# A buffer of its own for ScalarE's part of the last channel, 6144 of its columns on VectorE by integer range reduction and a monic polynomial, and the channels' outputs summed group by group

## The chip, the cores and the metric

The kernel runs on one core of a Trainium2 chip. The metric is the device time of one launch in microseconds. The kernel before took 3671.42 us (median of 3 runs, 3670.53 to 3673.81).

## The reference

An attention layer over 8 sequences of 512 rows and 128 features (16 heads of dimension 8), followed by a residual sum, layer norm and a feed-forward stage with a shared expert and eight selected experts. The attention repeats its softmax for 16 "wavelength" channels that share Q, K and V:

```python
def wl_step(acc, wl):
    cpm, iw = wl
    m = cpm[None, :, None, None]
    scores = jnp.einsum('bhqd,bhkd->bhqk', Q * m, K * m) * SCALE
    scores = scores * jnp.cos(KERR * scores * scores)
    attn = jax.nn.softmax(scores, axis=-1)
    out = jnp.einsum('bhqk,bhkd->bhqd', attn, V)
    return (acc + out * iw, None)
acc, _ = jax.lax.scan(wl_step, acc0, (cos_pm, interference_weights))
combined = acc / WL_CHANNELS
```

A channel differs from another only by a factor per head on the scores (cos squared, tile `c2`), so the kernel computes the scores of a head once and takes 16 exponentials of them with 16 scales. The cosine of the scores is 1 for these inputs; a flag computed at run time picks the branch without it.

## The kernel before, in words

The eight sequences are two groups of four (`g` = 0, 1). A **unit** `u` is one head of one group, so there are 32. Its scores lie transposed in `s_t[:, p, :]`, 128 partitions by 8192 columns (4 key tiles `kt` x 4 sequences x 512 queries), with `p = u % 2`; the row maximum is already in them. A unit has 16 **waves** `w`, one for each channel, and each engine walks through them in an order written out by hand, kept in step by counting semaphores.

- ScalarE (L583 to L598): for each wave one ACTIVATE Exp of `s_t` into `probs[:, w % 2, :]`, a ring of two buffers, with the channel's scale from a register. It waits until wave w-2's products are done (`pv_done`, L594). Of wave 15 it takes only columns 4096 to 8191.
- TensorE (L1188 to L1220): for each wave 16 matmuls (27 output rows for each of four sequences side by side, 512 columns) of `probs` with V. Three channels are a **group** `wg` and share a PSUM bank, so there are 6 groups, the last with one channel. `prep_pe` puts the next unit's work between the waves: its projections at step 1, row scores at 2 to 5, transposes at 6, the transposed scores at 8 to 11. `turn_products` transposes a group's products, one group late; it waits until the group before is weighted (`norm_done`).
- VectorE (L1378 to L1398): for a group's last wave the copy of its PSUM bank to `o_sb`; `prep_dve`, the other half of the next unit's preparation (copies, row maxima); `weigh(wg)`, which divides a group's products by their sums and multiplies by the channel's weight, into its place of `weighted` [P, 16, 128]; and at the unit's end one tensor_reduce over the 16 channels into `comb`.
- VectorE also computes exp for columns 0 to 4095 of wave 15, the **pieces** (`piece_dve`, L659): four pieces of 1024 columns (two sequences of a key tile), each by range reduction with the constant 1.5 x 2^23 and a polynomial of degree 6, in three parts that are laid at the steps in `PIECE_STEPS`. TensorE's `piece_pe` multiplies them with V into the last group's bank at steps 4, 8, 11, 15 (`PRODUCT_STEPS`). `piece_ready` and `piece_used` guard the one tile `x_p` that they share.
- In the second group of sequences (`g` = 1) the feed-forward stage for finished rows of the first is laid between the waves (`FF_STEPS`, steps counted over a pair of units): stages 1 to 3 at steps 12, 13, 15 of the even unit, stages 4 to 7 at steps 0, 7, 11, 12, 13 of the odd one. Stages 6 and 7 on TensorE wait for VectorE's stages 5.5 and 6.
- GpSimd copies the next unit's weights once per unit; SyncE issues the loads and stores. The second group's transposed x is stored early in DRAM from `x_next`, which lies in `weighted`, and loaded when the first group is through.

After the loop comes a tail: the rest of the feed-forward stage and the experts.

Of the kernel before, what the change touches and what calls it, by code (L numbers as in the profile page):

```python
# [6 lines left out]
ALU = mybir.AluOpType  # L7
ACT = mybir.ActivationFunctionType
AX = mybir.AxisListType
# [38 lines left out]
BIASED_MAGIC = float(1.5 * 2 ** 23 + 127)  # L48
LOWEST_Y = -126.0
EXP2 = (1.0000000005541674, 0.6931472057372656, 0.24022646890630472, 0.05550328776967869, 0.009618488957523083,  # L50
        0.00133999312182961, 0.00015345811891707452)
# [36 lines left out]
def postln_kernel(nc, a):  # L88
    with ExitStack() as ctx:
# [12 lines left out]
        weighted = sb("weighted", [P, W, GT * D])  # L102
        x_next = weighted[:].rearrange("p w n -> p (w n)")
# [105 lines left out]
        x_sq = sb("x_sq", [P, NT + 1])  # L209
# [15 lines left out]
        cos_small = sb("cos_small", [P, 3, NB])  # L225
# [8 lines left out]
        def products_of(wg):  # L234
# [11 lines left out]
                 "qa_ready st_done st_copied exp_done pv_done o_copied ot_done rz_done norm_done comb_done prep_chain chain "  # L246
# [306 lines left out]
        def _(act):  # L553
# [105 lines left out]
        def piece_dve(dve, piece, part, u, p, h):  # L659

            n = u * PIECES + piece
            link = Linked(dve, s["piece_chain"], n * PART_LINKS[3] + PART_LINKS[part])

            a = [c * (-1) ** i for i, c in enumerate(EXP2)]

            def horner(*coefficients):
                for c in coefficients:
                    link(nc.vector.scalar_tensor_tensor(out=x_p[:], in0=x_p[:], scalar=c, in1=x_y[:], op0=ALU.add, op1=ALU.mult))  # L668
# [21 lines left out]
        def piece_pe(pe, piece, u, p):  # L690

            pe.wait_ge(s["piece_ready"], u * PIECES + (piece + 1))
# [3 lines left out]
            kt, b0 = piece * X_BATCHES // NB, piece * X_BATCHES % NB  # L696
# [446 lines left out]
        def _(pe):  # L1143
# [28 lines left out]
            with pe.If(fast == 1):  # L1172
                for g in range(NG):
                    with pe.Fori(g * H // 2, (g + 1) * H // 2) as i:
                        for p in range(2):
# [12 lines left out]
                            for w in range(W):  # L1188
# [8 lines left out]
                                for kt in range(DVE_KT if w == W - 1 else 0, T):  # L1197
                                    for b in range(NB):
# [3 lines left out]
                                            probs[:, w % 2, at:at + S], start=(kt == 0 and w in FIRST_OF),  # L1202
# [40 lines left out]
        def _(dve):  # L1243
            nc.vector.memset(half_pi[:], float(np.pi / 2))
            nc.vector.memset(comb[:, NT - 3:NT - 1, :], 0.0).then_inc(s["sw3_zeroed"], 1)
# [68 lines left out]
            for step in range(W):  # L1314
# [4 lines left out]
                if step == 1:  # L1319
# [3 lines left out]
                    nc.vector.memset(r_z[:], 0.0).then_inc(s["pv_done"], 2)  # L1323
                    nc.vector.memset(loop_chunk.var, 0.0).then_inc(s["norm_done"], 1)
                    nc.vector.memset(loop_chunk.nt, 0.0).then_inc(s["y2_ready"], 1)
# [110 lines left out]
```

## Time and profile before

| | |
|---|---|
| median of 3 runs | 3671.42 us |
| profiled execution, its own time | 3674.77 us |
| its span | 3672.7 us, mean granted TensorE clock 0.882 |
| ScalarE busy | 3476.3 us (95%) |
| VectorE busy | 2934.6 us (80%) |
| TensorE matmuls busy | 2688.7 us (73%) |
| GpSimd busy | 55.8 us (2%) |

Busy shares are over the whole span. A row of a group gives the line, the engine, the operation, what is written and read, and how often. Where work is shown in order of time, neighbours of one kind are merged into one row, and the brackets give the engine's idle time ahead of it and what ended it.

### The profile page before, as it was taken

To read this page: it belongs to the slowest core of one execution; us is meant where nothing else is said; L and a number is where in the kernel's file an instruction comes from. 1 tells how busy PE (TensorE), PEld (TensorE's weight loads), DVE (VectorE), ACT (ScalarE), POOL (GpSimd) and SP (SyncE) were. 2 spreads that over 40 slices of the span, in tenths; PEclk is the share of its full clock that TensorE was granted. 3 is DMA by queue.
4 is the path that set the end of the run, shared out by engine and by line. 5 is a ranking of instruction groups with operands and counts; after the bars stand their busy time and mean duration, and the time that the engine had idled before them with its cause. 6 is when DMAs were issued, how large, how long until landed. Compare 5 with 4: busy or idle time off the path is not lost.

```text
span 3672.7 us, 50238 instructions
## 1 busy us (share of the span) xinstructions
PE 2688.7 (73%) x19639; PEld 823.7 (22%) x19639; DVE 2934.6 (80%) x3858; ACT 3476.3 (95%) x635; POOL 55.8 (2%) x206
## 2 busy tenths in 40 slices
PE   5777777777777777777777777777777777777673
PEld 2222222222222222222222222222222222222222
DVE  6788777788777788777788888788888888888787
ACT  6999999999999999999999999999999999999971
POOL 0000000000000000000000000000000000000000
PEclk7988988888889889888889898889888888988986
DMA  1000000000000000000000000000000000000000
GB/s 46 1 1 1 1 1 1 1 1 1 1 1 1 1 1 1 1 14 1 1 2 1 4 2 4 2 4 1 2 4 2 4 2 1 4 2 4 2 26 29
DMA packets 19221, 16.65 MB, mean 5 GB/s; under 512 B 4177, under 2 KB 16866, under 8 KB 18722
## 3 DMA queue, kind: packets, MB, share of 16 engines
q1 hardware_dynamic: 18130, 12.54, 1.2%
q8 instruction: 185, 3.03, 0.3%
q14 instruction: 58, 0.48, 0.0%
q10 hardware_dynamic: 720, 0.34, 0.0%
q0 software_dynamic: 128, 0.26, 0.0%
HBM read 7.76 MB, written 5.37 MB: 4 GB/s over the span
## 4 chain that ended last, share of the span: by engine, by line
ACT 53%; issue 27%; PE 9%; DVE 4%; ACTq 4%; DMA 0%; POOL 0%; DVEq 0%; POOLq 0%
ACT probs L597 53%; PE psum L1200 7%; ACTq L590 3%; DVE x_p L668 1%; PE psum L719 1%; DVE m_pad L770 0%; ACTq L594 0%; DVE x_p L686 0%; DVE probs L843 0%; PE psum L699 0%; DVE probs L1106 0%; DVE q_s L654 0%; DVE q_t L762 0%; ACT probs L614 0%; DVE k_s L654 0%
## 5 line engine op out<-in xcount | busy, mean ns | idle before, releaser
L597 ACT ACTIVATE probs<-s_t 128x8192 f32<-128x8192 f32 (+1 forms) x512 | 3440.8, 6807 | 69.2 <-PE psum L1200 67.6
L1200 PE MATMUL psum<-probs,v_pad 128*27 128x512 f32 x15872 | 2239.1, 691 | 578.7 <-ACT probs L597 523.0
L1200 PEld LDWEIGHTS psum<-probs,v_pad 128*27 128x27 f32 x15872 | 568.4, 119 | 1976.5 <-issue 1382.2
L668 DVE SCALAR_TENSOR_TENSOR x_p<-x_p,x_y 128x1024 f32<-128x1024 f32 x640 | 782.0, 1222 | 14.2
L1385 DVE COPY o_sb<-psum 128x512 f32<-128x512 f32 x192 | 132.7, 691 | 249.9 <-PE psum L1200 237.5
L791 DVE COPY s_t<-psum 128x2048 f32<-128x2048 f32 x130 | 297.0, 2284 | 11.2 <-PE psum L749 10.2
L770 DVE TENSOR_REDUCE m_pad<-psum 128x4 f32<-128x2048 f32 x132 | 301.6, 2286 | 3.9
L699 PE MATMUL psum<-x_p,v_pad 128*27 128x512 f32 x512 | 157.1, 696 | 190.1 <-DVE x_p L686 190.1
L761 DVE TENSOR_SCALAR v_t<-psum,b_head 128x512 f32<-128x512 f32 x33 | 24.8, 751 | 208.1 <-PE psum L719 208.1
L686 DVE SCALAR_TENSOR_TENSOR x_p<-x_p,x_2k 128x1024 f32<-128x1024 f32 x128 | 156.8, 1225 | 4.4
L1184 PE MATMUL psum<-ident,o_sb 128*128 128x128 f32 x768 | 122.1, 282 | 47.9 <-DVE weighted L1373 47.9
L679 DVE SCALAR_TENSOR_TENSOR x_y<-x_p,x_y 128x1024 f32<-128x1024 f32 x128 | 156.0, 1219 | 0.0
L1395 DVE TENSOR_REDUCE comb<-weighted 128x2048 f32 x32 | 121.3, 3792 | 5.2 <-DVE weighted L1373 5.2
L675 DVE TENSOR_SCALAR x_p<-x_y 128x1024 f32<-128x1024 f32 x128 | 88.9, 695 | 38.3 <-PE psum L699 30.3
L1368 DVE RECIPROCAL r_z<-psum 128x48 f32<-128x48 f32 x192 | 80.6, 420 | 40.8 <-PE psum L1184 37.2
L729 PE MATMUL psum<-k_s,q_s 24*128 24x512 f32 x528 | 67.7, 503 | 62.2 <-DVE k_s L654 40.0
L1184 PEld LDWEIGHTS psum<-ident,o_sb 128*128 128x128 f32 x768 | 82.8, 140 | 104.7 <-issue 104.0
L1373 DVE TENSOR_TENSOR weighted<-psum,r_z 128x384 f32<-128x384 f32 x192 | 98.5, 513 | 6.7
L672 DVE TENSOR_SCALAR x_y<-s_t,c_last 128x1024 f32<-128x1024 f32 x128 | 95.3, 744 | 1.6 <-issue 1.3
L719 PE MATMUL psum<-x_group,w_head 128*32 128x512 f32 x792 | 92.8, 602 | 0.0
L681 DVE TENSOR_SCALAR x_p<-x_y 128x1024 f32<-128x1024 f32 x128 | 88.9, 695 | 4.4
L677 DVE TENSOR_SCALAR x_2k<-x_p 128x1024 int16<-128x1024 int16 x128 | 88.9, 694 | 4.4
(244 smaller groups left out, 990.8 us busy)
## 6 DMA issues: line engine op xcount, KB each, us to landing
x_next_dram<-weighted SPq DMA_DIRECT2D x1, 1024.0 KB, 3.9
x_group<-x_next_dram SPq DMA_DIRECT2D x1, 1024.0 KB, 4.9
loop_memory<-in_L_attn_x_dram SPq DMA_DIRECT2D x8, 128.0 KB, 2.1
x_dram<-loop_memory SPq DMA_DIRECT2D x8, 128.0 KB, 1.8
out_dram<-loop_memory SPq DMA_DIRECT2D x8, 128.0 KB, 1.8
x_dram<-probs SPq DMA_DIRECT2D x2, 512.0 KB, 3.6
out_dram<-probs SPq DMA_DIRECT2D x2, 512.0 KB, 3.6
s_t<-in_L_ffn_ew_dram SPq DMA_DIRECT2D x3, 256.0 KB
```

Source lines behind the costliest of these rows:

```text
L597: nc.scalar.activation(probs[:, w % 2, n0:], s_t[:, p, n0:], ACT.Exp, scale=scales[w % 2]).then_inc(s["exp_done"], 1)
L668: link(nc.vector.scalar_tensor_tensor(out=x_p[:], in0=x_p[:], scalar=c, in1=x_y[:], op0=ALU.add, op1=ALU.mult))
L679: link(nc.vector.scalar_tensor_tensor(out=x_y[:], in0=x_p[:], scalar=BIASED_MAGIC, in1=x_y[:], op0=ALU.subtract, op1=ALU.subtract))
L686: nc.vector.scalar_tensor_tensor(out=x_p[:], in0=x_p[:], scalar=a[0], in1=x_2k[:], op0=ALU.add, op1=ALU.mult).then_inc(s["piece_ready"], 1)
L699: last = nc.tensor.matmul(products_of(NWG - 1)[L * b:L * b + SLOTS * A, :], v_pad[:, p, b * T + kt, VPAD:VPAD + SLOTS * A], x_p[:, i * S:( ...
L719: last = nc.tensor.matmul(prep[L * b:L * b + L, i, :], w_head[:, p, i, :], x_group[:, b * S:(b + 1) * S], start=True, stop=True)
L770: nc.vector.tensor_reduce(m_pad[:, qt, :].rearrange("p (b l) -> p b l", l=L)[:, :, R_S:R_S + 1], banks(qt), AX.X, ALU.max, negate=True).th ...
L791: nc.vector.tensor_copy(s_t[:, p, kt * NB * S:(kt + 1) * NB * S], banks(kt).rearrange("p b q -> p (b q)")) \
L1184: last = nc.tensor.transpose(psum[:, 6, qt * P:(qt + 1) * P], o_sb[:, wg % 2, qt * P:(qt + 1) * P], ident[:])
L1200: last = nc.tensor.matmul(products_of(wg)[L * b:L * b + SLOTS * A, :], v_pad[:, p, b * T + kt, c0:c0 + SLOTS * A], probs[:, w % 2, at:at + ...
L1385: nc.vector.tensor_copy(o_sb[:, wg % 2, :], products_of(wg)).then_inc(s["o_copied"], 1)
L1395: nc.vector.tensor_reduce(comb[:, bass.ds(g * GT, GT), bass.ds((u - g * H) * D, D)].rearrange("p (b t) e -> p t b e", b=NB), weighted[:].r ...
```

## The change

- `DVE_KT` goes from 2 to 3 key tiles: VectorE takes columns 0 to 6143 of wave 15 and ScalarE the last 2048. There are three pieces of 2048 columns (a key tile of all four sequences), in five parts; TensorE takes them at steps 6, 12, 15.
- ScalarE's part of wave 15 goes to a tile of its own, `probs_last`, with no wait ahead of it, and has a bias `ln_k`. The 15 other waves use the ring of two by `(p + w) % 2`.
- A piece: `tensor_scalar` multiplies the scores by the scale, clamps and writes int16 (the rounding gives the integer part); the difference is the fraction; a second `tensor_scalar` makes the bits of 2^n; the polynomial of degree 5 has leading coefficient 1 (all others, and ScalarE's part by its bias, are scaled alike, and the division by the sum takes the factor out).
- `weigh` writes group 0 into `summed` and each later group into `weighted`, which is then added to `summed`; the unit's end adds the three slots.
- `x_next`, `x_sq` and `cos_small` move to other tiles, and the descriptor scratch is given as 4096.

```diff
-DVE_KT = 2
-X_BATCHES = 2
-X_COLS = X_BATCHES * S
-PIECES = DVE_KT * NB // X_BATCHES
+DVE_KT = 3
+X_COLS = NB * S
+PIECES = DVE_KT
...
-PART_LINKS = (0, 4, 7, 9)
-PIECE_STEPS = {0: (0, 0), 2: (0, 1), 3: (0, 2), 4: (1, 0), 5: (1, 1), 7: (1, 2), 8: (2, 0), 9: (2, 1), 10: (2, 2),
-               11: (3, 0), 12: (3, 1), 13: (3, 2)}
-PRODUCT_STEPS = {4: 0, 8: 1, 11: 2, 15: 3}
+LN_K = float(np.float32(-np.log(EXP2[5])))
+K_EXP2 = tuple(c * float(np.exp(LN_K)) for c in EXP2[:5])
+PART_LINKS = (0, 2, 3, 4, 5, 6)
+PIECE_STEPS = {0: (0, 0, 2), 2: (0, 2, 3), 3: (0, 3, 4), 4: (0, 4, 5),
+               5: (1, 0, 1), 7: (1, 1, 3), 8: (1, 3, 4), 10: (1, 4, 5),
+               11: (2, 0, 1), 12: (2, 1, 3), 13: (2, 3, 5)}
+PRODUCT_STEPS = {6: 0, 12: 1, 15: 2}
...
-        weighted = sb("weighted", [P, W, GT * D])
-        x_next = weighted[:].rearrange("p w n -> p (w n)")
+        probs_last = sb("probs_last", [P, (T - DVE_KT) * NB * S])
+        weighted = sb("weighted", [P, SLOTS, GT * D])
+        summed = sb("summed", [P, SLOTS, GT * D])
+        x_next = x_p[:]
+        x_n = x_2k[:].bitcast(I16)
+        ln_k = sb("ln_k", [P, 1])
...
-                                act.wait_ge(s["pv_done"], u * W + (w + 1))
-                                n0 = DVE_KT * NB * S if w == W - 1 else 0
-                                nc.scalar.activation(probs[:, w % 2, n0:], s_t[:, p, n0:], ACT.Exp,
+                                if w == W - 1:
+                                    nc.scalar.activation(probs_last[:], s_t[:, p, DVE_KT * NB * S:], ACT.Exp, bias=ln_k[:, 0:1],
+                                                         scale=scales[w % 2]).then_inc(s["exp_done"], 1)
+                                    continue
+                                act.wait_ge(s["pv_done"], u * W + (w + 2 if w > 1 else w + 1))
+                                nc.scalar.activation(probs[:, (p + w) % 2, :], s_t[:, p, :], ACT.Exp,
                                                      scale=scales[w % 2]).then_inc(s["exp_done"], 1)
...
             if part == 0:
-                scores = s_t[:, p, piece * X_COLS:(piece + 1) * X_COLS]
-                link(nc.vector.tensor_scalar(x_y[:], scores, c2_last[:, bass.ds(h, 1)], LOWEST_Y, ALU.mult, ALU.max))
+                dve.wait_ge(s["piece_ready"], n + 1)
+                link(nc.vector.tensor_scalar(x_n, scores, scale, LOWEST_Y, ALU.mult, ALU.max))
+                link(nc.vector.scalar_tensor_tensor(out=x_y[:], in0=scores, scalar=scale, in1=x_n, op0=ALU.mult, op1=ALU.subtract))
+            if part == 1:
+                nc.vector.tensor_scalar(x_n, x_n, 127.0, 128.0, ALU.add, ALU.mult)
                 dve.wait_ge(s["piece_used"], n + 1)
-                link(nc.vector.tensor_scalar(x_p[:], x_y[:], BIASED_MAGIC, None, ALU.add))
-                low_halves = x_p[:].bitcast(I16).rearrange("p (n o) -> p n o", o=2)[:, :, 0:1]
-                nc.vector.tensor_scalar(x_2k[:].bitcast(I16).rearrange("p (n o) -> p n o", o=1), low_halves, 7, None,
-                                        ALU.logical_shift_left)
-                link(nc.vector.scalar_tensor_tensor(out=x_y[:], in0=x_p[:], scalar=BIASED_MAGIC, in1=x_y[:],
-                                                    op0=ALU.subtract, op1=ALU.subtract))
-                link(nc.vector.tensor_scalar(x_p[:], x_y[:], a[6], None, ALU.mult))
-            if part == 1:
-                horner(a[5], a[4], a[3])
+                link(nc.vector.scalar_tensor_tensor(out=x_p[:], in0=x_y[:], scalar=K_EXP2[4], in1=x_y[:], op0=ALU.add, op1=ALU.mult))
             if part == 2:
-                horner(a[2], a[1])
-                nc.vector.scalar_tensor_tensor(out=x_p[:], in0=x_p[:], scalar=a[0], in1=x_2k[:],
+                horner(K_EXP2[3])
+            if part == 3:
+                horner(K_EXP2[2])
+            if part == 4:
+                horner(K_EXP2[1])
+                nc.vector.scalar_tensor_tensor(out=x_p[:], in0=x_p[:], scalar=K_EXP2[0], in1=x_2k[:],
                                                op0=ALU.add, op1=ALU.mult).then_inc(s["piece_ready"], 1)
...
-            for i in range(X_BATCHES):
-                b = b0 + i
-                last = nc.tensor.matmul(products_of(NWG - 1)[L * b:L * b + SLOTS * A, :], v_pad[:, p, b * T + kt, VPAD:VPAD + SLOTS * A],
-                                        x_p[:, i * S:(i + 1) * S], start=(kt == 0), stop=False)
+            for b in range(NB):
+                last = nc.tensor.matmul(products_of(NWG - 1)[L * b:L * b + SLOTS * A, :], v_pad[:, p, b * T + piece, VPAD:VPAD + SLOTS * A],
+                                        x_p[:, b * S:(b + 1) * S], start=(piece == 0), stop=False)
...
+                                dst = (weighted if wg else summed)[:, 0:n, :]
+                                dve.wait_ge(s["sum_done"], u * NWG + max(wg, 1))
                                 nc.vector.tensor_tensor(
-                                    weighted[:, w0:w0 + n, :].rearrange("p r (j d) -> p j r d", d=D), ot[:, :, :, 0:D],
+                                    dst.rearrange("p r (j d) -> p j r d", d=D), ot[:, :, :, 0:D],
                                     rz.rearrange("p j (r o) -> p j r o", o=1).broadcast_to([P, GT, n, D]),
                                     ALU.mult).then_inc(s["norm_done"], 1)
+                                if wg:
+                                    dve.wait_ge(s["norm_done"], n1 + 1)
+                                    nc.vector.tensor_tensor(summed[:, 0:n, :], summed[:, 0:n, :], dst, ALU.add) \
+                                        .then_inc(s["sum_done"], 1)
...
-                            nc.vector.tensor_reduce(
+                            dve.wait_ge(s["sum_done"], u * NWG + NWG)
+                            nc.vector.tensor_tensor(weighted[:, 0, :], summed[:, 0, :], summed[:, 1, :], ALU.add) \
+                                .then_inc(s["sum_done"], 1)
+                            dve.wait_ge(s["sum_done"], u * NWG + (NWG + 1))
+                            nc.vector.tensor_tensor(
                                 comb[:, bass.ds(g * GT, GT), bass.ds((u - g * H) * D, D)].rearrange("p (b t) e -> p t b e", b=NB),
-                                weighted[:].rearrange("p w (t b d) -> p t b d w", t=T, b=NB), AX.X, ALU.add) \
+                                weighted[:, 0, :].rearrange("p (t b d) -> p t b d", t=T, b=NB),
+                                summed[:, 2, :].rearrange("p (t b d) -> p t b d", t=T, b=NB), ALU.add) \
                                 .then_inc(s["comb_done"], 1)
+                            dve.wait_ge(s["comb_done"], u + 1)
```

## Rows read from the trace of the kernel before

**Rows 1.** The page, part 1: busy us (share of the span) xinstructions.

```profile
PE 2688.7 (73%) x19639; PEld 823.7 (22%) x19639; DVE 2934.6 (80%) x3858; ACT 3476.3 (95%) x635; POOL 55.8 (2%) x206
```

**Rows 2.** ScalarE's groups by shape: busy us, mean ns | idle before.

```profile
L597 ACT ACTIVATE probs<-s_t 128x8192 f32<-128x8192 f32 x480 | 3328.7, 7021 | 69.2 <-PE psum L1200 67.6 <-DVE s_t L791 1.6
L597 ACT ACTIVATE probs<-s_t 128x4096 f32<-128x4096 f32 x32 | 115.3, 3602 | 0.0
...
L561 ACT ACTIVATE probs<-probs,half_pi 128x256 f32<-128x256 f32 x1 | 0.5, 508 | 2.7 <-DVE probs L1259 2.7
L634 ACT ACTIVATE probs<-probs 128x256 f32<-128x256 f32 x1 | 0.4, 416 | 10.2 <-DVE probs L1019 10.2
```

**Rows 3.** ScalarE in order of time: start us, us, work [idle before <-releaser].

```profile
51.25 13.96 ACT L597 ACTIVATE probs<-s_t 128x8192 f32<-128x8192 f32 x2 [1.55 <-DVE s_t L791]
...
1692.27 107.45 ACT L597 ACTIVATE probs<-s_t 128x8192 f32<-128x8192 f32 x16 [1.78 <-PE psum L1200]
...
2132.59 27.81 ACT L597 ACTIVATE probs<-s_t 128x8192 f32<-128x8192 f32 x4 [1.77 <-PE psum L1200]
...
2176.59 65.93 ACT L597 ACTIVATE probs<-s_t 128x8192 f32<-128x8192 f32 x10 [2.14 <-PE psum L1200]
...
3494.60 65.91 ACT L597 ACTIVATE probs<-s_t 128x8192 f32<-128x8192 f32 x10 [0.66 <-PE psum L1200]
3573.53 0.60 ACT L607 ACTIVATE probs<-psum 128x512 f32<-128x512 f32 x1 [13.02 <-PE psum L804]
```

**Rows 4.** ScalarE's waits: us in total, times, longest us.

```profile
ACT probs L597 <- PE psum L1200: 67.6, 43, 2.1
```

**Rows 5.** TensorE in order of time at a unit boundary, columns as in rows 3.

```profile
1687.04 5.57 PE L1200 MATMUL psum<-probs,v_pad 128*27 128x512 f32 x34 [3.29 <-ACT probs L597]
...
1692.88 1.89 PE L1200 MATMUL psum<-probs,v_pad 128*27 128x512 f32 x12
...
1696.86 0.63 PE L1184 MATMUL psum<-ident,o_sb 128*128 128x128 f32 x4 [1.50 <-DVE weighted L1373]
1699.43 5.33 PE L1200 MATMUL psum<-probs,v_pad 128*27 128x512 f32 x32 [1.95 <-ACT probs L597]
1706.28 3.64 PE L1200 MATMUL psum<-probs,v_pad 128*27 128x512 f32 x32 [1.52 <-ACT probs L597]
```

**Rows 6.** Stretches of one unit: us, PE, PEld, DVE, ACT, POOL busy, clock, DMA.

```profile
1692.27:1801.49 109.22, 81.89 (x604) 24.05 (x600) 84.45 (x92) 107.44 (x16) 0.74 (x5) 0.89 0.00 1
...
3122.59:3231.76 109.17, 82.19 (x610) 24.52 (x606) 89.21 (x119) 107.47 (x17) 2.53 (x8) 0.89 0.02 5
3231.76:3341.05 109.29, 83.08 (x615) 25.36 (x611) 94.61 (x145) 107.66 (x18) 0.74 (x5) 0.89 0.00 1
```

**Rows 7.** VectorE in order of time, two stretches.

```profile
1692.27 0.69 DVE L1385 COPY o_sb<-psum 128x512 f32<-128x512 f32 x1 [8.26 <-PE psum L1200]
...
2210.34 2.29 DVE L791 COPY s_t<-psum 128x2048 f32<-128x2048 f32 x1 [1.90 <-PE psum L749]
...
2244.49 0.68 DVE L1385 COPY o_sb<-psum 128x512 f32<-128x512 f32 x1
```

**Rows 8.** VectorE's groups by shape: busy us, mean ns | idle before.

```profile
L668 DVE SCALAR_TENSOR_TENSOR x_p<-x_p,x_y 128x1024 f32<-128x1024 f32 x640 | 782.0, 1222 | 14.2
...
L791 DVE COPY s_t<-psum 128x2048 f32<-128x2048 f32 x130 | 297.0, 2284 | 11.2 <-PE psum L749 10.2
...
L1395 DVE TENSOR_REDUCE comb<-weighted 128x2048 f32 x32 | 121.3, 3792 | 5.2 <-DVE weighted L1373 5.2
L672 DVE TENSOR_SCALAR x_y<-s_t,c_last 128x1024 f32<-128x1024 f32 x128 | 95.3, 744 | 1.6 <-issue 1.3
...
L677 DVE TENSOR_SCALAR x_2k<-x_p 128x1024 int16<-128x1024 int16 x128 | 88.9, 694 | 4.4
...
L1373 DVE TENSOR_TENSOR weighted<-psum,r_z 128x384 f32<-128x384 f32 x160 | 89.2, 558 | 5.6
...
L1373 DVE TENSOR_TENSOR weighted<-psum,r_z 128x128 f32<-128x128 f32 x32 | 9.3, 291 | 1.1
```

More of the change, by code:

```diff
@@ L208, in postln_kernel @@
         flag = sb("flag", [P, 1], I32)
-        x_sq = sb("x_sq", [P, NT + 1])
+        x_sq = x_y[:, 0:NT + 1]
         bound = probs[:, 1, 4 * W * H:]
@@ L245, in postln_kernel @@
                  "c2_step cos_done x_turned x_copied staged proj_done qkv_ready scores_done max_done mrow_done "
-                 "qa_ready st_done st_copied exp_done pv_done o_copied ot_done rz_done norm_done comb_done prep_chain chain "
+                 "qa_ready st_done st_copied exp_done pv_done o_copied ot_done rz_done norm_done sum_done comb_done prep_chain chain "
                  "ffw_turned ffw_ready xr_loaded xb_ready cs_ready x1_ready x1_stored y2_ready out_stored "
@@ L661, in piece_dve @@
             n = u * PIECES + piece
[L662 to L668, printed above, removed]
-            if part == 0:
-                scores = s_t[:, p, piece * X_COLS:(piece + 1) * X_COLS]
-                link(nc.vector.tensor_scalar(x_y[:], scores, c2_last[:, bass.ds(h, 1)], LOWEST_Y, ALU.mult, ALU.max))
-                dve.wait_ge(s["piece_used"], n + 1)
-                link(nc.vector.tensor_scalar(x_p[:], x_y[:], BIASED_MAGIC, None, ALU.add))
-                low_halves = x_p[:].bitcast(I16).rearrange("p (n o) -> p n o", o=2)[:, :, 0:1]
-                nc.vector.tensor_scalar(x_2k[:].bitcast(I16).rearrange("p (n o) -> p n o", o=1), low_halves, 7, None,
-                                        ALU.logical_shift_left)
-                link(nc.vector.scalar_tensor_tensor(out=x_y[:], in0=x_p[:], scalar=BIASED_MAGIC, in1=x_y[:],
-                                                    op0=ALU.subtract, op1=ALU.subtract))
-                link(nc.vector.tensor_scalar(x_p[:], x_y[:], a[6], None, ALU.mult))
@@ L682, in piece_dve, with horner @@
-            if part == 1:
-                horner(a[5], a[4], a[3])
-            if part == 2:
-                horner(a[2], a[1])
-                nc.vector.scalar_tensor_tensor(out=x_p[:], in0=x_p[:], scalar=a[0], in1=x_2k[:],
+            link = Linked(dve, s["piece_chain"], n * PART_LINKS[5] + PART_LINKS[part])
+            scores = s_t[:, p, piece * X_COLS:(piece + 1) * X_COLS]
+            scale = c2_last[:, bass.ds(h, 1)]
+            def horner(c):
+                link(nc.vector.scalar_tensor_tensor(out=x_p[:], in0=x_p[:], scalar=c, in1=x_y[:], op0=ALU.add, op1=ALU.mult))
@@ L1201, in _ @@
                                             products_of(wg)[L * b:L * b + SLOTS * A, :], v_pad[:, p, b * T + kt, c0:c0 + SLOTS * A],
-                                            probs[:, w % 2, at:at + S], start=(kt == 0 and w in FIRST_OF),
+                                            probs[:, (p + w) % 2, at:at + S] if w < W - 1 else probs_last[:, b * S:(b + 1) * S],
+                                            start=(kt == 0 and w in FIRST_OF),
                                             stop=(kt == T - 1 and w in LAST_OF))
@@ L1244, in _ @@
             nc.vector.memset(half_pi[:], float(np.pi / 2))
+            nc.vector.memset(ln_k[:], LN_K).then_inc(s["piece_ready"], 1)
             nc.vector.memset(comb[:, NT - 3:NT - 1, :], 0.0).then_inc(s["sw3_zeroed"], 1)
@@ L1322, in _ @@
                     nc.vector.memset(v_pad[:], 0.0)
-                    nc.vector.memset(r_z[:], 0.0).then_inc(s["pv_done"], 2)
+                    nc.vector.memset(r_z[:], 0.0).then_inc(s["pv_done"], 3)
                     nc.vector.memset(loop_chunk.var, 0.0).then_inc(s["norm_done"], 1)
+                    nc.vector.memset(summed[:], 0.0).then_inc(s["sum_done"], 1)
                     nc.vector.memset(loop_chunk.nt, 0.0).then_inc(s["y2_ready"], 1)
@@ L1372, in weigh @@
                                 dve.wait_ge(s["rz_done"], n1 * 2)
+                                dst = (weighted if wg else summed)[:, 0:n, :]
+                                dve.wait_ge(s["sum_done"], u * NWG + max(wg, 1))
                                 nc.vector.tensor_tensor(
-                                    weighted[:, w0:w0 + n, :].rearrange("p r (j d) -> p j r d", d=D), ot[:, :, :, 0:D],
+                                    dst.rearrange("p r (j d) -> p j r d", d=D), ot[:, :, :, 0:D],
                                     rz.rearrange("p j (r o) -> p j r o", o=1).broadcast_to([P, GT, n, D]),
                                     ALU.mult).then_inc(s["norm_done"], 1)
+                                if wg:
+                                    dve.wait_ge(s["norm_done"], n1 + 1)
+                                    nc.vector.tensor_tensor(summed[:, 0:n, :], summed[:, 0:n, :], dst, ALU.add) \
+                                        .then_inc(s["sum_done"], 1)
                             for w in range(W):
                                 if w in PIECE_STEPS:
-                                    piece_dve(dve, *PIECE_STEPS[w], u, p, u - g * H)
+                                    piece, part0, part1 = PIECE_STEPS[w]
+                                    for part in range(part0, part1):
+                                        piece_dve(dve, piece, part, u, p, u - g * H)
                                 if w in LAST_OF:
                                     wg = LAST_OF[w]
-                                    dve.wait_ge(s["pv_done"], u * W + (w + 3))
+                                    dve.wait_ge(s["pv_done"], u * W + (w + 4))
                                     nc.vector.tensor_copy(o_sb[:, wg % 2, :], products_of(wg)).then_inc(s["o_copied"], 1)
@@ L1422 @@
     from concourse.bass_utils import run_bass_kernel_spmd as _run
-    nc = _bacc.Bacc("TRN2", target_bir_lowering=False, num_devices=1)
+    nc = _bacc.Bacc("TRN2", target_bir_lowering=False, num_devices=1, dynamic_dma_scratch_size=4096)
     arrays, args = {}, {}
```

11 lines of the change are left out of this document (4 added, 7 removed).

## The prediction

> **What bounds the kernel now.** I read the page's shares of busy time first: ScalarE is busy for 95% of the span, VectorE for 80%, TensorE for 73% [rows 1]. Then ScalarE's groups by shape, which say what fills it: 480 exponentials of 8192 columns at 7.02 us and 32 of 4096 columns at 3.60 us, 3444 us in all [rows 2]. Then ScalarE's work in order of time [rows 3]. A unit (one head of one batch group, 16 waves) is there a run of 15 long exponentials and a short one: 107.45 us without a gap, with an idle gap of 1.78 us ahead of it, and the unit lasts 109.22 us [rows 3, 6]. As 107.45 less the short one's 3.60 is 103.85, the next long exponential starts 6.92 us after the one before (neighbours overlap by 0.10). The waits of ScalarE on TensorE are 67.6 us in 43 cases [rows 4]: 31 are the gaps at the unit boundaries, the others lie inside units, such as the 2.14 us ahead of the seventh exponential of an odd unit of the second half [rows 3].
>
> So ScalarE sets the pace, and the gap is the one place in each unit where it stands still. Why it does is seen in TensorE's order of work at that place [rows 5]: wave 14 begins at 1687.04, when its exponential is done, and is through about 1692.0 (the row's 5.57 us hold the first two records of the last wave too). The short exponential hides only 3.5 us of these 5, and the next one overwrites wave 14's buffer. Waves of 16 matmuls take 3.64 or 5.33 us in these rows, the long ones while the array runs at the lower of its two levels (1.2 GHz instead of 2.4) for a part of them; the mean granted clock of a unit is 0.89 [rows 6].
>
> VectorE has room: 84.5 us of 109.2 in a unit of the first half, 89.2 and 94.6 in the even and odd units of the second, where the feed-forward steps are added [rows 6]. But its idle time isn't free everywhere: in odd units of the second half it runs from step 9 to step 14 without a pause, from 2210.34 to 2244.49, and is ready for the copy of wave 14's products just as TensorE delivers them [rows 7].
>
> **ScalarE's part.** The last wave's exponential falls from 4096 to 2048 columns. From 8192 to 4096 columns costs 3.42 us [rows 2], so 2048 columns are 1.71 us. It gains a bias that is a column of SBUF. The nearest rows are an ACTIVATE with such a bias and one without, 508 and 416 ns for 256 columns (another function) [rows 2]: +0.09 us, between 0 and 0.09. I take 0.09, and the short one at 1.98 us. Saved: 1.62 us a unit.
>
> **The buffer.** The last wave no longer uses the ring of two, so the first exponential of the next unit needs wave 13 (long done) and not wave 14. The gap goes, with the 0.10 of overlap that it costs. Period of a unit with no wait: 103.85 + 1.98 less 0.10 = 105.73, against 109.22; 3.49 less. What is late next: the exponential after it needs wave 14, and the third one the next unit's wave 0. Put the end of exponential 14 at 0. Wave 14 ends at 5.2 at most; three quarters of the last wave now come from VectorE's pieces, and what is left for TensorE behind wave 14 is 4 + 4 matmuls, about 1.9 us: 7.1. The transposes of the last group follow 2.1 us after the last wave's matmuls (1694.77 to 1696.86 [rows 5]; VectorE copies and weights in between): 9.2, ended at 9.8, wave 0 at 13.5 or 15.2. The third exponential wants it at 1.9 + 13.9 = 15.8. So nothing waits in a unit of the first half.
>
> **VectorE's pieces.** Before, four of 1024 columns: 744 + 695 + 694 + 1219 + 695 + 5 x 1222 + 1225 ns = 11.4 us each, 45.5 a unit ([rows 8]; the two of 695 and those of 1219 and 1225 are forms of the kind and size shown). After, three of 2048: two tensor_scalar and six scalar_tensor_tensor. From 512 to 2048 columns a one-per-cycle form grows by 1.04 ns a column (691 ns for wave products, row at 1692.27; 2284 for 2048 [rows 7, 8]), so a scalar_tensor_tensor is 1222 + 1062 = 2.28 us. The tensor_scalar at 1024 columns costs about half of that a column, 0.52 ns, so the first, with its pointer scalar, is 744 + 535 = 1.28 and the shift of the exponent 1.23. A piece is 16.2, a unit 48.6: +3.1. No row shows a tensor_scalar from f32 to int16; the bounds are the two rates: at one column per cycle the first would take 2.33, the other 2.28, +2.1 a piece. I take the fast rate for both, as the strided int16 form has it (694 ns for 1024 [rows 8]).
>
> The Trainium skill ("VectorE: DVE Perf Modes", the tier table, and "Vector Engine (DVE) Microarchitecture Reference", section 5.1) has single-source operations between SBUF tensors at two results a cycle whatever the type, which the 694 ns row agrees with, and at four where all is 16 bits and dense, which no row here shows. By that the shift would take 0.69 us and the time below would come out at 3572.
>
> **The sums.** The tensor_reduce of 3.79 us goes. Four additions of 384 columns (558 ns, taken from the multiplication of that size [rows 8]) and three of 128 (291) come: 3.1. Net -0.7, so VectorE does 2.4 us more a unit: 86.9, 91.6 and 97.0 of a period of 105.7. It doesn't become the bound by its sum.
>
> **Where it does bind.** Odd units of the second half. The stretch from the copy at step 9 to the copy at step 14 was 34.15 us [rows 7]. In it, the pieces' parts were 3.65 + 4.18 + 3.77 + 3.65 = 15.25. Now they are 4.56 (end of piece 1) + 3.60 (start of piece 2) + 5.83 + 6.88 = 20.87, and two group sums add 1.12: 40.9. It begins when wave 9 and the scores behind it are done: 77.75 after the unit's start before [rows 3, 7], 75.5 without the 2.2 of the wait inside that unit, 1.7 sooner when wave 9 runs at the full clock. With 75.5 the copies begin at 116.4. The first takes 0.6, the way from there to the last transposes 2.1, these 0.63, wave 0 of the next unit 3.64: 123.4. The third exponential wants it at 105.73 + 13.94 = 119.7. A new wait of 3.7 us; 2.0 if wave 9 was fast, 5.4 if wave 0 is slow. Seven such boundaries count (the eighth odd unit is followed by the tail): 26 us. In the even units the feed-forward steps behind step 11 are about 5 us shorter, and the same sum ends a little before 119.7: no wait.
>
> **What else moves.** Piece 0 is now wanted at wave 6, not 4, so the 2.14 us waits inside odd units, which came from it, should go. Piece 1 (done about 84, wanted 88) and piece 2 (107 against 109, in units of the first half) stay hidden; if the conversions run at the slow rate piece 2 is just on time there. VectorE's new wait on its own comb result covers nothing that runs elsewhere. The store of the second half's x comes from another tile at the same place in SP's queue; POOL's queue is untouched. One more memset of 384 columns, 0.5 us ahead of the loop. The tail starts when the last unit is summed: ScalarE's exponential 14 of it ends at 3494.60 + 65.91 - 3.50 = 3557.0, its first tail copy starts at 3573.5 [rows 3]. That 16.5 stays: the last unit's chain is later by some 4, but the final reduction gives back 3 and the boundary's own chain 1.
>
> **The sum.** From the first exponential (51.25) to the end of exponential 14 of the last unit are 3505.8 us, = 31 x 109.22 + 103.9 + 16 of other waits. After: 31 x 105.73 + 103.9 + 2 (waits of the first two units, which lie before any of this) = 3383.6: -122. New waits +26, memset +0.5: -95.5. The profiled execution took 3674.8 for a span of 3672.7, so 3579.3; it stood 3.4 above the median of the runs, so 3576.
>
> **Rivals.**
> A, the above: 3576, with its own range of 3564 to 3588. 45%.
> B, no new waits: wave 9 ends early in every unit, or the shift is cheap, and VectorE's overrun is absorbed. 3550. For it: the margin is 2 to 3% of a unit. Against: the chain above has no idle time in the rows. 20%.
> C, conversions to or on int16 at one column per cycle: 2.1 us more in the binding stretch, 15 in all at the seven boundaries, and up to 1 at the eight even ones: 3599. 20%. For it: no row of that form.
> D, the boundary's wait only moves: from the first exponential to the third, because TensorE's round trips with VectorE (weighting, transposes) take longer than worked out. Then each unit gives only the 1.6 of the shorter exponential: 31 x 1.6 + 14 = 64, 3607 to 3610. Also the answer if the buffers' order doesn't free the first exponential from wave 14. Against it: 1 to 2.5 us of slack by the rows. 10%.
> E, slower. TensorE's clock. At 3.64 us a wave fits into 6.92; with the array at the lower level throughout it takes 7.28 and doesn't. A mean grant of 0.89 means 22% of the time at the lower level, so the 81.9 us of work in a unit [rows 6] are 67 at the full clock and 134 at the lower. They exceed 109.2 when 63% of the work runs there, three times today's share; all of it would give 134 us a unit and some 4400 in all. Against it: TensorE gets the same work in less time. 4%. One per cent is left for a new wait that happens to eat all.
>
> No change can be told from a difference below 0.2%, 7 us. Faster 94%, same 2%, slower 4%. The range reaches from B to beyond C: 3545 to 3608.
>
> **What would show it.** Right: 480 long exponentials still at 7.02 us, 32 short ones at 1.9 to 2.0; units of the first half at 105.7 us without a gap; gaps of 2 to 5 us ahead of the third exponential of even units in the second half, and VectorE without idle time from step 9 to 14 before them; scalar_tensor_tensor at 2.28, tensor_scalar at 1.2 to 1.3; seven small additions in place of the reduction. Wrong: a gap at every boundary (D), tensor_scalar at 2.3 (C), or waves on TensorE mostly above 5 us (E).

## The result, and the profile after

The changed kernel takes 3623.14 us (median of 4 runs, 3620.03 to 3626.35), the kernel before 3672.61 in the same session: a ratio of 0.9851, 95% interval 0.9827 to 0.9876. It is 1.5% faster. I had forecast 3576 and a range of 3545 to 3608; the sign was right, half of the gain didn't come, and the time lies 15 us above the range.

The profiled execution took 3620.03 us for a span of 3618.2, mean granted clock 0.898. The page's busy times, against [rows 1]:

```profile
PE 2562.4 (71%) x19639; PEld 757.6 (21%) x19639; DVE 2983.9 (82%) x3412; ACT 3421.4 (95%) x635; POOL 64.3 (2%) x206
```

ScalarE's two groups of exponentials, against [rows 2]:

```profile
L604 ACT ACTIVATE probs<-s_t 128x8192 f32<-128x8192 f32 x480 | 3328.8, 7025 | 64.6 <-PE psum L1203 63.1 <-DVE s_t L794 1.6
L600 ACT ACTIVATE probs_last<-s_t,ln_k 128x2048 f32<-128x2048 f32 x32 | 63.8, 1994 | 0.0
```

The short one is 1.99 us, as worked out. But the idle time on TensorE is 63.1 us, where [rows 4] had 67.6: the waits were to go, down to 28. They are fewer (15 for 43) and longer. ScalarE in order of time, two pairs of units, against [rows 3]:

```profile
368.85 1.98 ACT L600 ACTIVATE probs_last<-s_t,ln_k 128x2048 f32<-128x2048 f32 x1
370.74 103.93 ACT L604 ACTIVATE probs<-s_t 128x8192 f32<-128x8192 f32 x15
474.57 1.98 ACT L600 ACTIVATE probs_last<-s_t,ln_k 128x2048 f32<-128x2048 f32 x1
476.46 13.94 ACT L604 ACTIVATE probs<-s_t 128x8192 f32<-128x8192 f32 x2
493.71 90.11 ACT L604 ACTIVATE probs<-s_t 128x8192 f32<-128x8192 f32 x13 [3.32 <-PE psum L1203]
...
2189.41 13.94 ACT L604 ACTIVATE probs<-s_t 128x8192 f32<-128x8192 f32 x2
2210.60 90.11 ACT L604 ACTIVATE probs<-s_t 128x8192 f32<-128x8192 f32 x13 [7.26 <-PE psum L1203]
...
3499.43 1.99 ACT L600 ACTIVATE probs_last<-s_t,ln_k 128x2048 f32<-128x2048 f32 x1
3519.61 0.60 ACT L614 ACTIVATE probs<-psum 128x512 f32<-128x512 f32 x1 [18.19 <-PE psum L807]
```

The unit from 370.74 to 476.46 is 105.72 us long with no gap, as forecast. Every wait is in an even unit, ahead of its third exponential: 0.8 to 3.3 us in all eight of the first half (forecast: in the first one only), and 6.7 to 7.3 us in seven of the second (forecast: 3.7, at most 5.4). The tail's first copy starts 20.1 us after the end of the last unit's exponential 14, not 16.5.

TensorE in order of time (start us, us, work, idle before and its reason) at three boundaries, from an even to an odd unit and, in each half, from an odd to an even one, against [rows 5]:

```profile
378.15 0.63 PE L1187 MATMUL psum<-ident,o_sb 128*128 128x128 f32 x4 [1.52 <-DVE weighted L1381]
378.71 3.64 PE L1203 MATMUL psum<-probs,v_pad 128*27 128x512 f32 x32
...
483.87 0.63 PE L1187 MATMUL psum<-ident,o_sb 128*128 128x128 f32 x4 [1.52 <-DVE weighted L1381]
488.09 8.99 PE L1203 MATMUL psum<-probs,v_pad 128*27 128x512 f32 x64 [3.58 <-issue]
...
2198.55 1.04 PE L1187 MATMUL psum<-ident,o_sb 128*128 128x128 f32 x4 [3.26 <-DVE o_sb L1399]
2201.07 1.09 PE L1187 MATMUL psum<-ident,o_sb 128*128 128x128 f32 x4 [1.48 <-DVE weighted L1381]
2204.96 9.00 PE L1203 MATMUL psum<-probs,v_pad 128*27 128x512 f32 x64 [2.80 <-issue]
```

In the first, wave 0 follows the last transposes at once. In the two others TensorE stands between them for 3.58 and 2.80 us with `issue` as the reason: it waits for nothing that the profile shows. This is where its loop over pairs of units branches back (L1177 of the changed kernel). All such rows of this trace have 2.7 to 3.6 us. Then two waves take 9.0 us where two at 3.64 take 7.1 (neighbours overlap by 0.2), so one of them is slow: the granted clock is 0.63 from 2204.96 to 2210.30, and 1.00 in the wave at 378.71. At the boundaries with a branch the two waves take 8.4 to 10.0 us. The even unit that is entered by leaving the first loop and not by a branch back, at 1758.68, is the one without a wait. The kernel before had the same gap, and I read past it; a row of its TensorE at such a boundary, from the same view:

```profile
2249.06 0.63 PE L1184 MATMUL psum<-ident,o_sb 128*128 128x128 f32 x4 [1.50 <-DVE weighted L1373]
2253.30 8.82 PE L1200 MATMUL psum<-probs,v_pad 128*27 128x512 f32 x64 [3.61 <-issue]
```

The boundary that I took as the pattern [rows 5] leads from an even unit into an odd one. There is no branch in it.

VectorE's groups, against [rows 8]:

```profile
L674 DVE SCALAR_TENSOR_TENSOR x_p<-x_p,x_y 128x2048 f32<-128x2048 f32 x288 | 658.9, 2288 | 5.5
L678 DVE TENSOR_SCALAR x_2k<-s_t,c_last 128x2048 int16<-128x2048 f32 x96 | 123.0, 1281 | 32.8 <-issue 23.9 <-DVE comb L1412 8.9
L1387 DVE TENSOR_TENSOR summed<-summed,weighted 128x384 f32<-128x384 f32 x128 | 74.5, 582 | 4.4
L681 DVE TENSOR_SCALAR x_2k<-x_2k 128x2048 int16<-128x2048 int16 x96 | 66.1, 688 | 1.1
```

### The profile page after: what moved, and what is told of

The parts are those of the page before. It is cut to its first block, busy times and chain, and to the rows that moved or that the text cites. A ratio compares the mean times of both kernels' runs of the same rounds, so it can differ in the third digit from the quotient of the medians.

```text
span 3618.2 us, 49360 instructions
## 1 busy us (share of the span) xinstructions
PE 2562.4 (71%) x19639; PEld 757.6 (21%) x19639; DVE 2983.9 (82%) x3412; ACT 3421.4 (95%) x635; POOL 64.3 (2%) x206
## 4 chain that ended last, share of the span: by engine, by line
ACT 56%; issue 31%; ACTq 4%; PE 4%; DVE 2%; DMA 0%; POOL 0%; DVEq 0%; POOLq 0%
ACT probs L604 55%; ACTq L595 4%; PE psum L1203 3%; ACT probs_last L600 2%; ACTq L603 0%; DVE probs L846 0%; DVE x_p L674 0%; DVE probs L1109 0%; ACT probs L621 0%; PE psum L822 0%; PE psum L834 0%; PE psum L812 0%; DMA out_dram<-probs 0%; PE psum L817 0%; DVE probs L1022 0%
## 5 line engine op out<-in xcount | busy, mean ns | idle before, releaser
L604 ACT ACTIVATE probs<-s_t 128x8192 f32<-128x8192 f32 x480 | 3328.8, 7025 | 64.6 <-PE psum L1203 63.1
L1203 PE MATMUL psum<-probs,v_pad 128*27 128x512 f32 x15360 | 2016.6, 673 | 819.3 <-ACT probs L604 774.9
L1203 PEld LDWEIGHTS psum<-probs,v_pad 128*27 128x27 f32 x15360 | 485.9, 116 | 2139.7 <-issue 1224.5
L674 DVE SCALAR_TENSOR_TENSOR x_p<-x_p,x_y 128x2048 f32<-128x2048 f32 x288 | 658.9, 2288 | 5.5
L679 DVE SCALAR_TENSOR_TENSOR x_y<-s_t,c_last,x_2k 128x2048 f32<-128x2048 f32 x96 | 225.8, 2352 | 3.4
L691 DVE SCALAR_TENSOR_TENSOR x_p<-x_p,x_2k 128x2048 f32<-128x2048 f32 x96 | 220.0, 2292 | 3.3
L684 DVE SCALAR_TENSOR_TENSOR x_p<-x_y 128x2048 f32<-128x2048 f32 x96 | 219.5, 2286 | 0.0
L678 DVE TENSOR_SCALAR x_2k<-s_t,c_last 128x2048 int16<-128x2048 f32 x96 | 123.0, 1281 | 32.8 <-issue 23.9
L732 PE MATMUL psum<-k_s,q_s 24*128 24x512 f32 x528 | 67.6, 503 | 40.0 <-DVE k_s L661 33.8
L1387 DVE TENSOR_TENSOR summed<-summed,weighted 128x384 f32<-128x384 f32 (+1 forms) x160 | 83.9, 524 | 5.5
L1381 DVE TENSOR_TENSOR weighted<-psum,r_z 128x384 f32<-128x384 f32 (+1 forms) x160 | 80.7, 504 | 5.5
L782 DVE COPY v_pad<-psum 128x144 f32<-128x144 f32 x33 | 10.2, 309 | 81.9 <-PE psum L740 81.9
```

What stands on the lines that cost most here:

```text
L604: nc.scalar.activation(probs[:, (p + w) % 2, :], s_t[:, p, :], ACT.Exp, scale=scales[w % 2]).then_inc(s["exp_done"], 1)
L678: link(nc.vector.tensor_scalar(x_n, scores, scale, LOWEST_Y, ALU.mult, ALU.max))
L679: link(nc.vector.scalar_tensor_tensor(out=x_y[:], in0=scores, scalar=scale, in1=x_n, op0=ALU.mult, op1=ALU.subtract))
L684: link(nc.vector.scalar_tensor_tensor(out=x_p[:], in0=x_y[:], scalar=K_EXP2[4], in1=x_y[:], op0=ALU.add, op1=ALU.mult))
L1203: last = nc.tensor.matmul(products_of(wg)[L * b:L * b + SLOTS * A, :], v_pad[:, p, b * T + kt, c0:c0 + SLOTS * A], probs[:, (p + w) % 2, a ...
```

## The experiments

Theory T: TensorE's branch back stands between VectorE's last weighting and wave 0 of each even unit. With a short exponential of 2 us and no wait at the start of a unit, ScalarE comes to need wave 0 sooner than that. Theory V: in odd units of the second half VectorE's longer chain adds to it. The rival to T is that V alone makes the waits. Ratios are to the kernel before on the same chip.

**r1_rotate.** TensorE's loop is cut one wave later; `unit_part(g, i, p, w0, w1)` issues waves w0 to w1 - 1 of a unit.

```diff
-                    with pe.Fori(g * H // 2, (g + 1) * H // 2) as i:
-                        for p in range(2):
-                            u = i * 2 + p
...
+                CUT = 1
+                unit_part(0, 0, 0, 0, CUT)
+                for g in range(NG):
+                    with pe.Fori(g * H // 2, (g + 1) * H // 2 - g) as i:
+                        unit_part(g, i, 0, CUT, W)
+                        unit_part(g, i, 1, 0, W)
+                        unit_part(g, i + 1, 0, 0, CUT)
+                unit_part(1, H - 1, 0, CUT, W)
+                unit_part(1, H - 1, 1, 0, W)
```

> The changed kernel with TensorE's loop cut one wave later: its branch back comes after wave 0 of an even unit and not ahead of it; same instructions in the same order. Theory T (TensorE stands 2.8 to 3.6 us at the branch, this delays wave 0 of every even unit and with it ScalarE's third exponential): the waits of 0.8 to 3.3 us in even units of the first half go, those of 6.9 in the second half fall by 2.8 to 4.5 each; 34 to 45 us in all, 3578 to 3589 us. Rival V (VectorE's longer chain alone makes these waits, the branch is hidden beside it): less than 5 us, 3618 to 3625.

3582.12 us (3579.23 to 3582.86), ratio 0.9742 (0.9720 to 0.9764). T holds, V alone doesn't. In the first half no wait is left but that of the first unit; in the second 3.1 to 4.3 us are left of 6.7 to 7.3. TensorE at the boundary that answers to 2204.96:

```profile
2186.42 1.09 PE L1185 MATMUL psum<-ident,o_sb 128*128 128x128 f32 x4 [1.48 <-DVE weighted L1391]
2187.43 5.18 PE L1202 MATMUL psum<-probs,v_pad 128*27 128x512 f32 x32
2193.15 3.64 PE L1202 MATMUL psum<-probs,v_pad 128*27 128x512 f32 x32 [0.53 <-issue]
```

Wave 0 follows the transposes at once. The branch now lies behind it and costs the array 0.53 us, and 0.5 to 1.1 us in the five rows of this trace that show it: most of it passes while wave 0 runs. Without the stand, wave 0 takes 3.64 us at five of the seven boundaries of the first half where the changed kernel has a branch. So the stand and the slow wave behind it went together there; whether the one makes the other, no run shows.

**r2_ff24.** VectorE's feed-forward stage 5.5 goes to where VectorE had 2.75 us of idle time, ahead of the copy at step 9. VectorE in the changed kernel, at both ends of its stretch without a pause:

```profile
2157.16 2.29 DVE L794 COPY s_t<-psum 128x2048 f32<-128x2048 f32 x1 [2.75 <-PE psum L752]
...
2197.81 1.28 DVE L1399 COPY o_sb<-psum 128x512 f32<-128x512 f32 x2
```

```diff
-FF_STEPS = {12: 1, 13: 2, 15: 3, 16: 4, 23: 5, 27: 5.5, 28: 6, 29: 7}
+FF_STEPS = {12: 1, 13: 2, 15: 3, 16: 4, 23: 5, 24: 5.5, 28: 6, 29: 7}
```

> The changed kernel with feed-forward stage 5.5 of VectorE (5 us) moved from step 11 of the odd unit to step 8, ahead of a place where VectorE waits some 3 to 4 us for TensorE. Theory T+V (VectorE's chain from step 9 to the unit's end adds to the branch): the 6.9 us waits of the second half fall by 3 to 4.5 us each, those of the first half stay; 7 x 3.5 and as much in front of the tail: 28 us, 3595 us (3588 to 3602). If the branch alone made the waits: no change.

3598.56 us (3596.65 to 3601.37), ratio 0.9790 (0.9769 to 0.9812): 24.6 less than the changed kernel, within what was expected. The waits of the second half fall to 3.6 to 5.3 us, by 2.6 on average and not by the 3 to 4.5 expected; those of the first stay at 0.6 to 3.2, the wait ahead of the tail falls from 18.2 to 14.8.

**r3_both.** Both edits.

> Both edits. T+V: the two parts of each wait add, so almost none is left: 60 to 68 us below the changed kernel, 3555 to 3563 us. If the two hide each other the sum of the two single gains is not reached.

3564.23 us (3561.27 to 3565.66), ratio 0.9692 (0.967 to 0.9713). 58.9 less than the changed kernel; the single gains are 41.0 and 24.6, 65.6 together. So the two parts add, but for 7 us, and the time lies 1 us above the range expected. It beats both kernels. ScalarE's waits on wave products in it:

```profile
ACT probs L604 <- PE psum L1202: 11.5, 10, 1.9
```

About 4 of the 7 us lie in the tail, behind the loop. From ScalarE's first tail copy to the span's end the profiled executions of r1 and r5 take 94.5 and 94.4 us, all others 98 to 99. One addition on VectorE makes the difference, here with GpSimd's work beside it, in the changed kernel and in r1:

```profile
3544.14 6.16 DVE L1105 TENSOR_TENSOR probs<-probs 128x1024 f32<-128x1024 f32 x1 [0.48 <-ACT probs L583]
3544.30 4.91 POOL L493 TENSOR_TENSOR probs<-probs,rows 128x512 f32<-128x512 f32 x4
...
3508.92 1.23 DVE L1105 TENSOR_TENSOR probs<-probs 128x1024 f32<-128x1024 f32 x1 [0.48 <-ACT probs L583]
3509.74 5.65 POOL L493 TENSOR_TENSOR probs<-probs,rows 128x512 f32<-128x512 f32 x4
```

It takes 1.23 us in r1 and r5, where GpSimd's four operations start 0.82 and 0.68 us behind it, and 5.8 to 6.7 us in the eight other traces, where they start between 0.15 ahead and 0.67 behind. No run varies this alone, and which of the unprofiled executions had the short tail is not known. So a difference of some 4 us between two runs need not come from the edit.

**r4_ring.** The own buffer undone.

```diff
+                                act.wait_ge(s["pv_done"], u * W + (w + 2))
                                 if w == W - 1:
-                                    nc.scalar.activation(probs_last[:], s_t[:, p, DVE_KT * NB * S:], ACT.Exp, bias=ln_k[:, 0:1],
+                                    nc.scalar.activation(probs[:, 1, DVE_KT * NB * S:], s_t[:, p, DVE_KT * NB * S:], ACT.Exp, bias=ln_k[:, 0:1],
...
-                                act.wait_ge(s["pv_done"], u * W + (w + 2 if w > 1 else w + 1))
-                                nc.scalar.activation(probs[:, (p + w) % 2, :], s_t[:, p, :], ACT.Exp,
+                                nc.scalar.activation(probs[:, w % 2, :], s_t[:, p, :], ACT.Exp,
```

> The changed kernel with the own buffer undone: ScalarE's part of the last wave goes back to the ring of two, w % 2, and the waits count as before. Theory: the exponential at a unit's start waits for wave 14 again, now 3.3 to 3.5 us as the short one covers only 1.9 of its 5.2, in all 31 boundaries; of the waits ahead of the third exponential those of the first half go and 3.5 of each 6.9 stay. 130 us of waits in place of 63: 3685 to 3695 us, slower than the kernel before. Rival: the buffer was worth only the 1.8 us gap of the kernel before: 3660 to 3670.

3684.00 us (3678.31 to 3689.24), ratio 1.0027 (1.0014 to 1.0040): slower than the kernel before, by a little. ScalarE in order of time:

```profile
1468.59 103.94 ACT L604 ACTIVATE probs<-s_t 128x8192 f32<-128x8192 f32 x15 [3.39 <-PE psum L1203]
1577.82 103.94 ACT L604 ACTIVATE probs<-s_t 128x8192 f32<-128x8192 f32 x15 [3.40 <-PE psum L1203]
```

The units of the first half start 109.23 us apart, as in the kernel before: what the exponential lost in columns, the wait for wave 14 took. In all ScalarE waits 128.3 us for wave products, for 130 expected; in the second half the waits ahead of the third exponential are 3.7 to 6.5 us and not 3.4. The time is 1 us below the range expected. Without the buffer, shifting the columns is worth nothing, with the new arithmetic and the group sums in place.

**r5_own4096.** The other half alone: the buffer without the shift of columns.

```diff
-DVE_KT = 3
-X_COLS = NB * S
-PIECES = DVE_KT
+DVE_KT = 2
+X_COLS = 2 * S
+PIECES = DVE_KT * 2
...
+PIECE_STEPS = {0: (0, 0, 2), 2: (0, 2, 4), 3: (0, 4, 5), 4: (1, 0, 2), 5: (1, 2, 4), 7: (1, 4, 5),
+               8: (2, 0, 2), 9: (2, 2, 4), 10: (2, 4, 5), 11: (3, 0, 2), 12: (3, 2, 4), 13: (3, 4, 5)}
+PRODUCT_STEPS = {4: 0, 8: 1, 11: 2, 15: 3}
```

> The changed kernel without the shift of columns: ScalarE keeps 4096 columns of the last wave in its own buffer (with the bias), VectorE takes 4096 in four pieces of 1024 with the new arithmetic, laid at the steps of the kernel before; group sums as in the change. A unit without waits is 103.85 + 3.69 - 0.10 = 107.4 us, 1.7 more than changed, but the short exponential covers 1.7 us more of the boundary and VectorE's pieces cost 34 us and not 49. Theory T+V: the waits ahead of the third exponential fall to 0 to 2 us in both halves, so what the columns cost ScalarE they give back in waits: 3605 to 3620 us, no slower than the changed kernel. Rival (the shorter exponential is worth its 1.7 us a unit whatever follows): 3623 + 31 x 1.7 = 3670 to 3680.

3610.76 us (3609.21 to 3611.56), ratio 0.9825 (0.9807 to 0.9843): by the medians 12 us less than with the shift, and within what was expected. The intervals of the two ratios overlap, and 4 us of this profiled execution are the short tail, so that it is faster isn't shown. The rival, 3670 to 3680, is out. Its ScalarE groups and waits:

```profile
L603 ACT ACTIVATE probs<-s_t 128x8192 f32<-128x8192 f32 x480 | 3327.8, 7020 | 11.3 <-PE psum L1204 9.6 <-DVE s_t L795 1.6
L599 ACT ACTIVATE probs_last<-s_t,ln_k 128x4096 f32<-128x4096 f32 x32 | 118.2, 3694 | 0.0
```

ScalarE has 54 us more to do (118.2 for 63.8) and waits 53 less for wave products (9.6 for 63.1). The tail starts 5.4 us sooner (12.5 us of wait ahead of its first copy for 18.2) and is itself 4 us shorter. The bias costs 92 ns (3694 for 3602 without, in [rows 2]).

**r6_before_rotate.** The cut of r1 in the kernel before.

> The kernel before with TensorE's loop cut after wave 0 of the even unit. Theory T: there the next unit starts 1.8 us later and behind a short exponential of 3.5 us, wave 0 is done in time even behind the branch, so nearly nothing moves: -10 to +2 us, 3662 to 3674. Rival (the branch costs its 3 us on the path in any kernel): 15 x 3 = 45 us less, 3625.

3688.28 us (3683.73 to 3690.14), ratio 1.0038 (1.0023 to 1.0054). The rival falls: the branch was hardly on the path there. But the time lies outside my range too: I expected no loss, and there are some 14 us. The waits show where; ScalarE on wave products, here and, as its total, in [rows 4]:

```profile
ACT probs L597 <- PE psum L1199: 79.4, 49, 2.1
```

Six waits and 12 us more. Ten of the 12 us stand ahead of the seventh exponential of odd units, 2.14 us in all eight of the second half; in the kernel before, three of these have as much, and the others less or none. Ahead of the seventh exponential of the even ones there are 4 us more. Gone are three waits ahead of the third exponential, 0.3, 0.3 and 1.5 us, the only ones in the second half of the kernel before: so much of the branch was on the path. The wave in question is wave 4, which comes behind a late piece and is a slow one there (5.6 us for 30 of its 32 records at 1948.00). That the cut has shifted how TensorE's work falls against its clock is my reading; no run shows it.

**r7_rot_less.** r1_rotate, less VectorE work: one Horner step of each piece is left out.

```diff
-PART_LINKS = (0, 2, 3, 4, 5, 6)
+PART_LINKS = (0, 2, 3, 4, 4, 5)
...
-            if part == 3:
-                horner(K_EXP2[2])
```

> r1_rotate with one Horner step left out of each piece (the third coefficient is not used): VectorE has 2.3 us less in each of three pieces, two of them (step 8 and the end of step 13) by the chain of an odd unit in question; one lies behind its last pause. Theory V: the 3.1 to 4.3 us waits of r1_rotate in the second half fall by about 2.3 each and the start of the tail by as much: 18 us less, 3564 (3560 to 3570); first half unchanged. Rival (these waits are TensorE's): no change from 3582.

3564.84 us (3562.32 to 3568.04), ratio 0.9698 (0.9681 to 0.9716): 17.3 less than r1 by the medians, 16 by the ratios. The waits of the second half fall to 1.0 to 3.6 us, by 1.7 on average, and the wait ahead of the tail by 2.4 (18.5 to 16.1); the first half keeps none. V holds: of the 2.3 us that were taken out of VectorE's stretch from step 9 on (the step that was left out of piece 2; that of piece 1 lies at step 8, ahead of VectorE's pause), most comes off each wait in the second half. In the first half nothing moves.

**r8_own4096_rot.** r5 with the cut of r1.

> r5_own4096 with TensorE's loop cut after wave 0 of the even unit, as in r1_rotate. The waits ahead of the third exponential in r5 (0.2 to 3.5 us, 9.6 in seven places) are the branch's, so they go: 10 us less, 3600 (3596 to 3604). The shift of columns is then worth 3600 - 3582 = 18 us with the branch moved, where it cost 12 with the branch in place; without the chain of VectorE in odd units of the second half it would be 31 x 1.7 = 53. Rival: the waits in r5 are from another source and stay, 3611.

3606.71 us (3601.85 to 3610.57), ratio 0.9825 (0.9803 to 0.9846). The waits on wave products fall from 9.6 to 1.7 us, in two places; so they were the branch's. The time missed its range of 3596 to 3604: the ratio is that of r5, the medians differ by 4. The traces say why: up to the first tail copy this execution is 9.2 us shorter than that of r5 (3505.06 for 3514.23), as expected, and its tail is 4.5 longer, with the slow addition that r5 has not. So with the branch out of the way the shift of columns is worth some 24 us by the medians (3606.7 to 3582.1) and 30 by the ratios. From the first exponential to the first tail copy it is 23.2 us (3454.2 to 3431.0), of the 53 of its 31 x 1.7: r1 has 24.5 us more of waits on wave products, nearly all in the second half, and 5.7 more ahead of the tail, and these are the rest.

## Why the prediction was wrong, by its own steps

- **ScalarE's part** was right: 1.994 us for 1.98, units of 105.72 for 105.73.
- **VectorE's prices** were right but for one: 2288 ns for 2.28, 1281 for 1.28; the shift of the exponent took 688 where I had taken 1.23 us. The Trainium skill ("VectorE: DVE Perf Modes", the tier table) has 0.69 us for 2048 columns of bf16; the measurement on int16 agrees. An addition took 582 ns, not 558. The stretch from step 9 to step 14 was 40.65 us for 40.9, from 2157.16 to 2197.81. It began 73.7 us after the unit's start, as with the fast wave 9 of my other case (75.5 less 1.7), and the last transposes came 3.3 us behind it, not 2.7, so they began at 117.6 for 119.1. Rival C is out.
- **The buffer** is the step that failed: "wave 0 at 13.5 or 15.2 ... So nothing waits in a unit of the first half." The way from the last transposes to wave 0 was taken as nothing, from a boundary where it is nothing. At every second one it holds TensorE's branch, 2.7 to 3.6 us, and behind it a slow wave, which the 15.2 had in it: 484.5 + 3.6 + 5.3 = 493.4, wanted at 490.4. r1, which takes the branch out of this way, takes 36.9 of the 63.1 us of waits with it. The same omission is in **Where it does bind**: from the unit's start, the transposes ended at 118.7 (119.7 by the forecast), and 2.8 + 5.3 behind them made 126.8 where 123.4 was forecast and 119.9 wanted. My upper end had the slow wave and not the branch. This is what rival D said in general, a wait moved from the first exponential to the third, but I put it down to the round trips with VectorE, and they took what I had worked out.
- **The sum.** Waits, each with its lost overlap of 0.1: 64.6 for 28, 36.6 more. The tail 3.6 later: I had set VectorE's lateness in the last unit (4) off against savings in the final reduction (3) and the boundary (1). The lateness came: the last transposes end 14.5 us after the end of exponential 14, and 10.7 before. The savings did not reach the tail, as TensorE's way out of the loop stands in it. TensorE before (two rows) and after:

```profile
3567.05 0.63 PE L1184 MATMUL psum<-ident,o_sb 128*128 128x128 f32 x4 [1.50 <-DVE weighted L1373]
3572.38 3.67 PE L804 MATMUL psum<-ident,comb 128*128 128x128 f32 x16 [4.70 <-DVE comb L1395]
...
3512.95 1.09 PE L1187 MATMUL psum<-ident,o_sb 128*128 128x128 f32 x4 [1.47 <-DVE weighted L1381]
3518.49 3.65 PE L807 MATMUL psum<-ident,comb 128*128 128x128 f32 x16 [4.45 <-issue]
```

  The result of the last head is ready at 3516.0, 2.5 us before TensorE goes on; before, it came at 3572.3, and TensorE went on at once. So 0.25 us are left of the 3. r2 takes 3.4 us off the wait ahead of the tail by relieving VectorE. Waits and tail together are 40.2 of the 40.7 between 3579.3 and the 3620.0 of the profiled execution. The other 6 are from the step to the median: before, the profiled execution lay 3.4 above the median of the runs, this time 3.1 below.
- **The split of the gain**: the buffer with the new arithmetic and the group sums gives 65 us (r5), the shift with these and without the buffer loses 8 by the medians and 10 by the ratio (r4), all together give 49 as changed, 94 with r1's cut and 112 with both edits. What the arithmetic and the sums are worth by themselves no run shows.
- **E** was right to be small: the mean grant rose from 0.882 to 0.898. Its working has a slip: 22% is the share of the time at the lower level, and I used it as a share of the work. By the time, 81.9 us of work are 73 at the full clock and 146 at the lower (an estimate from [rows 6]), and they exceed 109.2 when half of the work runs there.

## What to carry to other kernels

When work is taken from the engine that sets the pace, everything that used to hide behind it has to be laid end to end again, and `issue` gaps at a loop's branch belong into that chain. A gap is named after what ended it last, so look at all boundaries of a kind and not at one. Cut an engine's loop where its queue still holds work: the same 3 us of branch cost 37 us of waits (41 us of time) at one place and next to nothing one wave later. That holds for the kernel at hand: the same cut in the kernel before gave nothing and lost 14 us.

## What the runs showed of the hardware

- A branch back in a long loop: TensorE stands 2.7 to 3.6 us (changed kernel) and 3.1 to 3.6 (kernel before) where it had waited for VectorE just before, and 0.5 to 1.1 us (r1) where a wave of matmuls lay ahead of it. VectorE stands 3.1 to 3.4 us at its own in the second half of the changed kernel.
- `tensor_scalar` from f32 to int16 in SBUF, 2048 columns: 1281 ns; int16 to int16: 688 ns.
- A bias column costs an ACTIVATE 92 ns (3694 for 3602 at 4096 columns, and 508 for 416 at 256 in [rows 2]).
- An addition of 1024 columns on VectorE took 1.23 us in two traces and 5.8 to 6.7 in eight, with GpSimd at work beside it.
